# Routing statistics by groups of four tiles in a macaron MoE and attention block

## The chip, the cores and the metric

The kernel runs on one core of one Trainium2 chip. The metric is the device time of one execution in microseconds. PE is TensorE, DVE is VectorE, ACT is ScalarE, POOL is GpSimd, SP is SyncE; SP and ACT also issue DMAs.

## The reference

4096 tokens of width 256 go through a macaron block: x + 0.5 FFN(norm x), then x + attention(norm x), then x + 0.5 FFN(norm x) again with the same weights. The norm has no weights:

```python
m = jnp.mean(x, axis=axis, keepdims=True)
v = jnp.var(x, axis=axis, keepdims=True)
return (x - m) / jnp.sqrt(v + eps)
```

The FFN is a mixture of experts: sigmoid scores over 8 experts from a gate, the top 2 with weights normalised and scaled by 2.5, each expert a gated SiLU network with 176 hidden units, and a shared network of 352 hidden units on every token.

```python
scores = jax.nn.sigmoid(xf @ gate_w.T)
topk_w, topk_idx = jax.lax.top_k(scores, TOP_K)
shared_out = jax.nn.silu(xf @ shared_wg.T) * (xf @ shared_wu.T) @ shared_wd.T
```

## The kernel before

The tokens stand in SBUF as X, 32 tiles of 128 tokens. Each of the two feed-forward parts has three stages with barriers between them: front_stage (routing), expert_stage, combine_stage. The attention lies between the two parts. The change is in front_stage, so it acts twice, from 18.7 us and from 983.9 us of the span.

When front_stage begins, the statistics ST of every tile (bn_stats) are there. The stage turns them into means and variances MV (bn_aggr), adds EPS, takes the square root on ScalarE (L355, in place in RSTD) and the reciprocal on VectorE. Then it works on groups of four tiles, q = 0 to 7:

- normalise(q), VectorE, L476: four tensor_scalar write the normalised tiles into XN. XN has two buffers, so from q = 2 on it waits until TensorE has transposed group q - 2 (xT_done) and until that group's DMA to DRAM has landed (xn_out).
- transpose_x(q, j), TensorE, L650: two tiles each into PSUM. It waits for x_low of the group before (xl_done).
- x_high(q, j), ScalarE, L361, rounds the transposed tiles to fp32r; x_low(q, j), VectorE, L482, takes the remainder.
- keep_xn(q), L366, is a DMA that ScalarE issues behind x_high(q, 1): 512 KB of normalised tiles to DRAM for the expert stage.
- logits(q), turn_logits(q) on TensorE and copy_logits(q) on ScalarE (L373) make the gate's scores, with the gate's weights split by VectorE into GWhl and GWh0 (L457 to L461).
- up(w, m), silu(w, m) (L381), gated_h(w, m) (L490), h_high(w, m) (L393), h_low compute the shared network for the first two groups, one chunk of 128 hidden units in each turn of the loop from q = 2 on (q = 3 on for h_high).
- expert_high(n) (L400, L402) on ScalarE and expert_low(n) (L331) on GpSimd split the experts' weights; L426, L428 and L317, L321 do the same for the shared weights. SP's load of expert n waits until expert_low(n - 2) is done.

Each engine runs its own list in the order in which it is written, and a wait in the list holds all that stands behind it on that engine. ScalarE's list is, for each q: h_high(q - 3), x_high(q, 0), x_high(q, 1), keep_xn(q), copy_logits(q - 1), at q = 1 the shared weights, from q = 2 on expert_high(q - 2) and silu(q - 2). VectorE's list: gate weights, all 32 bn_aggr, add, reciprocal, normalise(0), normalise(1), constants() (L508 to L513, a few casts, OFF, and a memset), and then for each q: x_low(q, 0), x_low(q, 1), normalise(q + 2), at q = 5 h_low_2, from q = 2 on gated_h(q - 2). link(ins) makes VectorE wait until that instruction is done. OFF is read only by the combine stage.

Of the kernel before, what the change touches and what calls it, by code (L numbers as in the profile page):

```python
# [11 lines left out]
ALU = mybir.AluOpType  # L12
ACT = mybir.ActivationFunctionType
AX = mybir.AxisListType
F32 = mybir.dt.float32
# [12 lines left out]
EPS = 1e-5  # L28
# [96 lines left out]
def front_stage(nc, tag, S, X, ST, MV, ident, w_up, w_down, w_shared, gate, xn_dram,  # L125
# [6 lines left out]
    D, NT, NS, FF, E, NJ = S.D, S.NT, S.NS, S.FF, S.E, S.NJ  # L132
    FA, FB = S.FA, S.FB
    NG = NT * TOP_K
    NW = NT // 4
# [10 lines left out]
    with ExitStack() as c1:  # L146
# [12 lines left out]
        GW = sb("GW", [P, 2, E])  # L159
# [191 lines left out]

        @block.scalar
        def _(act):
            act.wait_ge(rstd_in, 1)
            nc.scalar.activation(RSTD[:, :], RSTD[:, :], ACT.Sqrt).then_inc(rstd_out, 1)  # L355

            def x_high(q, j):
                act.wait_ge(xT_done, 2 * q + j + 1)
                if q >= NF + 2:
                    act.wait_ge(lt_done, q - 1)  # L360
                nc.scalar.activation(x_part(0, q)[:, :, j * 2 * P:(j + 1) * 2 * P],  # L361
                                     ps_x[j][:, :].rearrange("p (c n) -> p c n", c=2), ACT.Copy).then_inc(xh_done, 1)

            def keep_xn(q):
                act.wait_ge(xn_ready, 4 * q + 4)
                act.dma_start(xn_dram[q * 4 * P:(q + 1) * 4 * P, :].rearrange("(i p) d -> p i d", p=P),  # L366
                              XN[:, q % 2, :, :]).then_inc(xn_out[q % 2], 16)

            def copy_logits(q):
                act.wait_ge(lt_done, q + 1)  # L370
                if q >= 2:
                    act.wait_ge(gate_done, q - 1)
                nc.scalar.activation(LT[0:2 * E, q % 2, :], ps_lt[q % 2][0:2 * E, :], ACT.Copy).then_inc(lt_copied, 1)  # L373

            def silu(w, m):
                n = HC * w + m
                act.wait_ge(up_done, 2 * n + 1)

                if n >= 2:
                    wait_low(n - 2)  # L380
                nc.scalar.activation(H[0:CHUNKS[m][1], n % 2, :], ps_u[2 * n % RING][0:CHUNKS[m][1], :],  # L381
                                     ACT.Silu).then_inc(silu_done, 1)

            def wait_low(n):
                if n % HC == 2:
                    act.wait_ge(hl_dve, n // HC + 1)
                else:
                    act.wait_ge(hl_pool, 2 * (n // HC) + n % HC + 1)

            def h_high(w, m):  # L390
                n = HC * w + m
                act.wait_ge(h_ready, n + 1)
                nc.scalar.activation(hs[0][0:CHUNKS[m][1], w, m, :], H[0:CHUNKS[m][1], n % 2, :],  # L393
                                     ACT.Copy).then_inc(hh_done, 1)

            def expert_high(n):
                e, b = n, n % 2
                block_free(act, e)
                act.wait_ge(expert_in[b], 16 * 3 * (n // 2 + 1))
                nc.scalar.activation(W[:, e, S.UH:S.UH + 4 * FF], raw[b][:, 0:4 * FF], ACT.Copy).then_inc(expert_hi, 1)  # L400
                for at_h, at, rows_n, to in ((S.AH, RA, FA, 0), (S.BH, RB, FB, 0), (S.BH, RB, FB, FB)):
                    nc.scalar.activation(W[to:to + rows_n, e, at_h:at_h + D], raw[b][0:rows_n, at:at + D],  # L402
                                         ACT.Copy).then_inc(expert_hi, 1)

            def token_ids(n):

                act.wait_ge(onehot, n + 1)
                if n >= 2:
                    act.wait_ge(tok_done, n - 1)
                for g in range(CH):  # L410
                    last = nc.scalar.activation(TSEL[:, n % 2, g, :], EQT[:, n % 2, g, :], ACT.Copy,
                                                scale=id_f[:, n * CH + g:n * CH + g + 1])
                last.then_inc(ids, 1)

            for q in range(NW):
                if q >= 3:
                    h_high(*divmod(q - 3, HC))
                x_high(q, 0)
                x_high(q, 1)
                keep_xn(q)  # L420
                if q >= 1:
                    copy_logits(q - 1)
                if q == 1:
                    act.wait_ge(shared_in, SHARED_IN)
                    for c in range(2):
                        nc.scalar.activation(WU[0][:, c, :, :], raw_up[:, c, :, :], ACT.Copy).then_inc(shared_hi, 1)  # L426
                    for m, (at, n) in enumerate(CHUNKS):
                        nc.scalar.activation(WS[0][0:n, m, :], raw_down[0:n, m, :], ACT.Copy).then_inc(shared_hi, 1)  # L428
                if q >= 2:
                    expert_high(q - 2)  # L430
                    silu(*divmod(q - 2, HC))
            h_high(NF - 1, HC - 1)
            copy_logits(NW - 1)
            act.wait_ge(gate_done, NW)
            act.wait_ge(shared_lo, 2 + HC)
            nc.scalar.activation(SC[:, :, :].rearrange("p t e -> p (t e)"), ps_gate[:, 0:E * NT],
                                 ACT.Sigmoid).then_inc(sig_done, 1)
            for n in range(NW - 2, E):
                expert_high(n)
            act.wait_ge(pre_done, 1)  # L440
            nc.scalar.activation(PRE[:, :], ps_count[:, 0, :], ACT.Copy).then_inc(pre_copied, 1)
            nc.scalar.activation(TOT[:, :], ps_count[:, 1, :], ACT.Copy).then_inc(pre_copied, 1)
            for n in range(8):
                token_ids(n)

        @block.vector
        def _(dve):
            count = [0]

            def link(ins):  # L450

                count[0] += 1
                ins.then_inc(chain, 1)
                dve.wait_ge(chain, count[0])

            dve.wait_ge(gate_in, 16)
            nc.vector.memset(GWh0[:, :, E:2 * E].bitcast(F32), 0.0)  # L457
            nc.vector.tensor_copy(GWh0[:, :, 0:E], GW[:, :, :])
            nc.vector.tensor_tensor(ADD[:, :], ident[0:2 * E, 0:E], ident[0:2 * E, E:2 * E], ALU.add)
            link(nc.vector.tensor_copy(GWhl[:, :, 0:E], GW[:, :, :]))  # L460
            nc.vector.tensor_tensor(GWhl[:, :, E:2 * E], GW[:, :, :], GWhl[:, :, 0:E].bitcast(F32),  # L461
                                    ALU.subtract).then_inc(gate_w, 1)
            for t in range(NT):
                last = nc.vector.bn_aggr(MV[:, t, :], ST[:, t, :])
            link(last)
            nc.vector.tensor_scalar(RSTD[:, :], MV[:, :, 1], EPS, None, ALU.add).then_inc(rstd_in, 1)
            dve.wait_ge(rstd_out, 1)
            link(nc.vector.reciprocal(RSTD[:, :], RSTD[:, :]))

            def normalise(q):  # L470
                if q >= 2:
# [34 lines left out]
            def constants():  # L506
                dve.wait_ge(consts, 6)
                link(nc.vector.tensor_copy(prio[:, :], prio_i[:, :]))  # L508
                link(nc.vector.tensor_copy(row_f[:, :], row_i[:, :]))
                link(nc.vector.tensor_copy(row_h[:, :], row_i[:, :]))  # L510
                link(nc.vector.tensor_copy(id_f[:, :], id_i[:, :, :].rearrange("p k t -> p (k t)")))
                nc.vector.scalar_tensor_tensor(OFF[:, :], MV[:, :, 0], -1.0, RSTD[:, :], ALU.mult, ALU.mult)
                nc.vector.memset(W[FB:2 * FB, :, S.BL:S.BL + D].bitcast(F32), 0.0).then_inc(cleared, 1)  # L513
                dve.wait_ge(cleared, 1)

# [76 lines left out]
            def one_hot(n):  # L592
                if n >= 2:
# [6 lines left out]
                                        RF[:, part].unsqueeze(2).to_broadcast([P, CH, P]),  # L600
                                        ALU.is_equal).then_inc(rows, 1)

            normalise(0)
            normalise(1)
            constants()
            for q in range(NW):
                x_low(q, 0)
                x_low(q, 1)
                if q + 2 < NW:
                    normalise(q + 2)  # L610
                if q == 5:
                    h_low_2(0)
                if q >= 2:
                    gated_h(*divmod(q - 2, HC))
# [28 lines left out]
        def _(pe):  # L643
# [72 lines left out]
                                            start=n == 0 and g == 0, stop=n == 7 and g == CH - 1)  # L716
                last.then_inc(tok_done, 1)

            pe.wait_ge(gate_w, 1)
            for q in range(NW):  # L720
                transpose_x(q, 0)
                transpose_x(q, 1)
                if q >= 1:
                    logits(q - 1)
                if q >= 2:
                    turn_logits(q - 2)
                if q == 2:
                    pe.wait_ge(shared_lo, 2)
                if q >= 2:
                    up(*divmod(q - 2, HC))  # L730
# [1392 lines left out]
```

## Time and profile before

| | us |
|---|---|
| median of three runs | 1339.91 |
| lowest, highest | 1338.66, 1339.95 |
| the profiled execution | 1341.68 |
| its span, first to last instruction | 1339.6 |
| TensorE, VectorE, ScalarE, GpSimd busy | 1163.8, 982.0, 793.1, 535.3 |

Times in rows are microseconds from the start of the span. Busy shares are means over stages with different limits; what matters for one stage is the order of its instructions in time and which wait ends last.

### The profile page before, as it was taken

Reading aid. Unit: us, or ns where it says so; the run is one execution under the profiler, and the core shown is the slowest. Engines: PE = TensorE matmul, PEld = TensorE weight load, DVE = VectorE, ACT = ScalarE, POOL = GpSimd, SP = SyncE. Lnnn points to the kernel's source line nnn. Section 1 sums busy time; section 2 is a strip of 40 time slices with the busy share of each in tenths; the row PEclk is TensorE's granted clock in tenths of the full one; section 3 lists DMA queues with packets and bytes.
Section 4 is the critical chain, followed back from the end, with each engine's and each line's share of the span. In section 5 each row is a group of like instructions: output and inputs, shape, how many; then the busy total and the mean of one; then the engine's idle time right before and its main releaser. Section 6 shows DMA issues by size and latency. Waiting matters only on the chain. (4 is left out here: it accounts for less than half of the span.)

```text
span 1339.6 us, 38859 instructions
## 1 busy us (share of the span) xinstructions
PE 1163.8 (87%) x13796; PEld 866.7 (65%) x13796; DVE 982.0 (73%) x2151; ACT 793.1 (59%) x1944; POOL 535.3 (40%) x738
## 2 busy tenths in 40 slices
PE   1873999989859969999998999999858659999897
PEld 1653999968748825555554555553746559999686
DVE  6666666648869879998887888893586766666586
ACT  1645666663226606877776777788636466666631
POOL 0642444337715512322332322333516334442576
PEclk9975999989969969999998999999979769999899
DMA  6320444423355651222221222210234114443354
GB/s 206 127 80 28 128 132 134 125 74 95 96 190 196 220 92 47 67 59 62 60 63 52 62 59 60 63 39 3 95 113 128 49 56 131 131 134 111 99 150 137
DMA packets 96384, 132.43 MB, mean 99 GB/s; under 512 B 15644, under 2 KB 81116, under 8 KB 96220
## 3 DMA queue, kind: packets, MB, share of 16 engines
q1 hardware_dynamic: 74716, 86.07, 21.4%
q0 software_dynamic: 13056, 35.67, 9.7%
q10 hardware_dynamic: 8448, 8.39, 1.8%
q8 instruction: 117, 1.92, 0.6%
q14 instruction: 47, 0.39, 0.1%
HBM read 81.35 MB, written 48.23 MB: 97 GB/s over the span
## 5 line engine op out<-in xcount | busy, mean ns | idle before, releaser
L1740 ACT ACTIVATE s_PR<-s_ps_b 128x512 f32<-128x512 f32 (+3 forms) x768 | 331.1, 496 | 123.2 <-PE s_ps_b L1851 118.1
L1760 DVE TENSOR_REDUCE s_MX<-s_ps_a 128x1 f32<-128x512 f32 (+3 forms) x608 | 357.9, 653 | 50.4 <-PE s_ps_a L1829 47.3
L1851 PE MATMUL s_ps_b<-QO,KO 99*32 99x512 bf16 (+3 forms) x3072 | 217.2, 329 | 8.1 <-issue 3.6
L1711 POOL TENSOR_SCALAR_AFFINE_SELECT s_PR<-s_PR 128x256 f32<-128x256 f32 x256 | 103.2, 406 | 301.7 <-ACT s_PR L1740 296.1
L792 POOL DMA_INDIRECT f_XG<-xn_scratch,f_tok_u x144 | 136.1, 945 | 206.2 <-PE f_ps_x L888 137.7
L1829 PE MATMUL s_ps_a<-KO,QO 96*32 96x512 bf16 (+3 forms) x3072 | 212.2, 338 | 1.4 <-DVE s_MX L1760 1.2
L1003 POOL DMA_INDIRECT f_YG<-y_scratch,f_slots_u x128 | 128.3, 1003 | 87.4 <-issue 33.8
L1868 PE MATMUL s_ps_o<-s_PR,s_VG 128*17 128x512 f32 (+3 forms) x1536 | 158.8, 488 | 1.0 <-POOL s_PR L1711 0.6
L898 PE MATMUL f_ps_u<-f_W,f_xh 128*128 x576 | 152.8, 348 | 0.0
L1851 PEld LDWEIGHTS s_ps_b<-QO,KO 99*32 99x32 bf16 x3072 | 81.3, 96 | 90.7 <-ACT s_PR L1740 44.4
L1829 PEld LDWEIGHTS s_ps_a<-KO,QO 96*32 96x32 bf16 x3072 | 81.2, 99 | 69.3 <-DVE s_MX L1760 24.6
L920 PE MATMUL f_ps_y<-f_W,f_hh 112*128 (+1 forms) x576 | 121.1, 303 | 0.6 <-DVE f_hh L852 0.4
L1824 PE MATMUL s_ps_a<-s_neg,s_identb 128*32 128x128 bf16 (+2 forms) x1408 | 92.5, 251 | 9.7 <-POOL s_identb L1676 9.4
L845 DVE TENSOR_TENSOR f_xl<-f_ps_x,f_xh 128x256 fp32r<-128x256 f32 x144 | 61.1, 424 | 51.9 <-ACT f_xh L817 51.9
L898 PEld LDWEIGHTS f_ps_u<-f_W,f_xh 128*128 128x128 f32 x576 | 95.4, 193 | 0.4 <-issue 0.4
L898 PE MATMUL f_ps_u<-f_W,f_xl 128*128 x288 | 94.3, 327 | 0.0
L864 DVE TENSOR_TENSOR f_H<-f_SG,f_ps_u 128x176 f32<-128x176 f32 x144 | 48.6, 338 | 58.0 <-ACT f_SG L832 58.0
L920 PEld LDWEIGHTS f_ps_y<-f_W,f_hh 112*128 112x128 f32 (+1 forms) x576 | 88.0, 190 | 1.6 <-issue 1.6
L832 ACT ACTIVATE f_SG<-f_ps_u 128x176 f32<-128x176 f32 x144 | 45.8, 318 | 67.8 <-PE f_ps_u L898 67.8
L811 ACT ACTIVATE f_YS<-f_ps_y 128x256 f32<-128x256 f32 x144 | 55.5, 386 | 37.2 <-PE f_ps_y L920 37.2
L888 PE MATMUL f_ps_x<-ident,f_XG 128*128 128x128 f32 x288 | 56.6, 279 | 11.8 <-DMA f_XG<-xn_scratch,f_tok_u 11.8
L650 PE MATMUL f_ps_x<-ident,f_XN 128*128 128x128 f32 x128 | 21.7, 317 | 50.3 <-DVE f_XN L476 33.9
(227 smaller groups left out, 2637.8 us busy)
## 6 DMA issues: line engine op xcount, KB each, us to landing
y_scratch<-f_YS SPq DMA_DIRECT2D x144, 128.0 KB, 1.7
qk_scratch<-p_QK SPq DMA_DIRECT2D x32, 384.0 KB, 3.1
QO<-qk_scratch SPq DMA_DIRECT2D x96, 128.0 KB, 2.8
KO<-qk_scratch SPq DMA_DIRECT2D x96, 128.0 KB, 2.8
xn_scratch<-f_XN ACTq DMA_DIRECT2D x16, 512.0 KB, 4.0
f_RAW<-in_w_up SPq DMA_DIRECT2D x16, 352.0 KB, 3.2
X<-in_x SPq DMA_DIRECT2D x4, 1024.0 KB, 9.4
x_scratch<-X SPq DMA_DIRECT2D x1, 4096.0 KB, 16.4
```

The source lines that it names most:

```text
L792: nc.gpsimd.indirect_dma_start(out=XG[:, j % 4, :], out_offset=None, in_=xn_dram[:, :], in_offset=bass.IndirectOffsetOnAxis(ap=tok_u[:, j: ...
L845: nc.vector.tensor_tensor(xs[1][:, k % 2, :], ps_x[k % 2][:, 0:D], xs[0][:, k % 2, :].bitcast(F32), ALU.subtract).then_inc(xl_done, 1)
L898: last = nc.tensor.matmul(ps_u[k % 2][:, 0:2 * FF], xs[a][:, k % 2, c * P:(c + 1) * P], W_at[:, ds(offset + ((S.UL if b else S.UH) + c * 2 ...
L920: last = nc.tensor.matmul(ps_y[b][:, 0:D], h, W_at[0:h.shape[0], ds(offset + at, D)], start=i == 0, stop=i == len(plan) - 1)
L1003: nc.gpsimd.indirect_dma_start(out=YG[:, t % RING, c, :], out_offset=None, in_=y_dram[:, :], in_offset=bass.IndirectOffsetOnAxis(ap=slots_ ...
L1711: nc.gpsimd.affine_select(out=tile, in_=tile, compare_op=ALU.is_ge, fill=0.0, base=0, pattern=[[0, 2], [1, P]], channel_multiplier=-1)\
L1740: nc.scalar.activation(PR[:, u // 2 % SLOTS, u % 2, 0:W - lo], ps_b[u % RING][:, lo:W], ACT.Exp, scale=SCALE).then_inc(exp_done, 1)
L1760: nc.vector.tensor_reduce(MX[:, h:h + heads, i, s], ps_a[slot][:, 0:heads * keys].rearrange("p (h n) -> p h n", h=heads), AX.X, ALU.max).t ...
L1824: nc.tensor.matmul(scores[strip, :, keys - P:keys], identb[:, strip], neg[:, 0:heads, :], start=True, stop=False, skip_group_check=True)
L1829: last = nc.tensor.matmul(ps_a[slot][strip, at:at + keys], QO[k][0:R, h, i * P + strip.start:i * P + strip.stop], KO[k][0:R, h, s * W:s * ...
L1851: last = nc.tensor.matmul(ps_b[u % RING][strip, lo:W], KO[k][0:RM, h, i * P + strip.start:i * P + strip.stop], QO[k][0:RM, h, hf * W + lo: ...
L1868: last = nc.tensor.matmul(ps_o[32 * h:32 * h + V1, lo:W], VG[k][:, i, h * V1:(h + 1) * V1], PR[:, (2 * n + h // 2) % SLOTS, h % 2, 0:W - l ...
```

## The change

The aggregations, the added EPS, the square root and the reciprocal are done for four tiles at a time: measure(q) on VectorE, deviation(q) on ScalarE, invert(q) on VectorE. Groups 0 and 1 are measured before the first normalisation. The gate's weights are prepared behind normalise(0) and group 2 is measured behind them; groups 3 to 7 are measured inside the loop, behind x_low(q, 1): group 3 at q = 0, groups 4 and 5 at q = 1, groups 6 and 7 at q = 2. ScalarE takes deviations 0 and 1 ahead of its loop, deviation 2 at q = 0, 3 and 4 at q = 1, 5, 6 and 7 at q = 2, each time behind x_high(q, 1) and ahead of keep_xn(q). TensorE waits for the gate's weights behind the transposes of q = 1 and no longer at its start. OFF is computed at q = 6 and no longer in constants().

```diff
 @block.scalar
+            def deviation(q):
+                act.wait_ge(rstd_in, q + 1)
+                cols = RSTD[:, 4 * q:4 * q + 4]
+                nc.scalar.activation(cols, cols, ACT.Sqrt).then_inc(rstd_out, 1)
-            act.wait_ge(rstd_in, 1)
-            nc.scalar.activation(RSTD[:, :], RSTD[:, :], ACT.Sqrt).then_inc(rstd_out, 1)
...
+            deviation(0)
+            deviation(1)
             for q in range(NW):
...
                 x_high(q, 0)
                 x_high(q, 1)
+                for n in ((2,), (3, 4), (5, 6, 7))[q] if q < 3 else ():
+                    deviation(n)
                 keep_xn(q)
 @block.vector
+            def measure(q):
+                tiles = range(4 * q, 4 * q + 4)
+                for t in tiles:
+                    last = nc.vector.bn_aggr(MV[:, t, :], ST[:, t, :])
+                link(last)
+                nc.vector.tensor_scalar(RSTD[:, 4 * q:4 * q + 4], MV[:, 4 * q:4 * q + 4, 1], EPS, None,
+                                        ALU.add).then_inc(rstd_in, 1)
+            def invert(q):
+                dve.wait_ge(rstd_out, q + 1)
+                cols = RSTD[:, 4 * q:4 * q + 4]
+                link(nc.vector.reciprocal(cols, cols))
...
-                nc.vector.scalar_tensor_tensor(OFF[:, :], MV[:, :, 0], -1.0, RSTD[:, :], ALU.mult, ALU.mult)
...
+            measure(0)
+            measure(1)
+            invert(0)
             normalise(0)
+            gate_weights()
+            measure(2)
+            invert(1)
             normalise(1)
             constants()
             for q in range(NW):
                 x_low(q, 0)
                 x_low(q, 1)
+                for n in ((3,), (4, 5), (6, 7))[q] if q < 3 else ():
+                    measure(n)
                 if q + 2 < NW:
+                    invert(q + 2)
                     normalise(q + 2)
+                if q == NW - 2:
+                    nc.vector.scalar_tensor_tensor(OFF[:, :], MV[:, :, 0], -1.0, RSTD[:, :], ALU.mult, ALU.mult)
 @block.tensor
-            pe.wait_ge(gate_w, 1)
             for q in range(NW):
                 transpose_x(q, 0)
                 transpose_x(q, 1)
+                if q == 1:
+                    pe.wait_ge(gate_w, 1)
```

gate_weights() holds the five instructions of L457 to L461 with their wait for the gate's DMA.

## Rows read from the trace of the kernel before

**Rows 1.** Timeline, VectorE, first routing stage: start us, us, instruction, idle before and its releaser.

```profile
20.57 0.15 DVE L458 CAST f_GWh<-f_GW 128x16 fp32r<-128x16 f32 x1 [2.37 <-issue]
...
20.99 2.21 DVE L464 BATCH_NORM_AGGREGATE MV<-ST 128x2 f32<-128x6 f32 x32
...
23.71 0.35 DVE L468 RECIPROCAL f_RSTD<-f_RSTD 128x32 f32<-128x32 f32 x1 [0.29 <-ACT f_RSTD L355]
24.10 2.67 DVE L476 TENSOR_SCALAR f_XN<-X,MV,f_RSTD 128x256 f32<-128x256 f32 x8
...
27.63 0.19 DVE L512 SCALAR_TENSOR_TENSOR f_OFF<-MV,f_RSTD 128x32 f32<-128x32 f32 x1
28.29 1.76 DVE L513 MEMSET f_W<- 64x2048 f32 x1 [0.47 <-issue]
30.09 1.29 DVE L482 TENSOR_TENSOR f_W<-f_ps_x,f_W 128x512 fp32r<-128x512 f32 x2
31.66 1.38 DVE L476 TENSOR_SCALAR f_XN<-X,MV,f_RSTD 128x256 f32<-128x256 f32 x4 [0.29 <-DMA xn_scratch<-f_XN]
```

**Rows 2.** Timeline, ScalarE and its DMA queue (ACTq), same stage.

```profile
18.68 1.28 ACT L355 ACT_TABLE_LOAD   x1 [18.68 <-PEq L2059]
...
26.10 0.60 ACT L361 ACTIVATE f_W<-f_ps_x 128x512 fp32r<-128x512 f32 x1 [2.43 <-PE f_ps_x L650]
...
26.96 0.40 ACTq L366 DMA_DIRECT2D xn_scratch<-f_XN  x1
...
32.91 0.37 ACTq L366 DMA_DIRECT2D xn_scratch<-f_XN  x1
34.47 0.59 ACT L373 ACTIVATE f_LT<-f_ps_y 16x512 f32<-16x512 f32 x1 [0.97 <-PE f_ps_y L661]
...
35.35 0.37 ACTq L366 DMA_DIRECT2D xn_scratch<-f_XN  x1
```

**Rows 3.** DMA issues at 18.68, 26.96 and 32.91: count, KB, us to landing.

```profile
f_GW<-in_gate SPq DMA_DIRECT2D x1, 8.0 KB, 1.8
...
xn_scratch<-f_XN ACTq DMA_DIRECT2D x1, 512.0 KB, 4.6
...
xn_scratch<-f_XN ACTq DMA_DIRECT2D x1, 512.0 KB, 2.9
```

**Rows 4.** Timeline, GpSimd and VectorE, 35.9 to 45.8 us.

```profile
35.89 3.38 POOL L317 TENSOR_TENSOR f_WUl<-f_RAWS,f_WUh 128x704 fp32r<-128x704 f32 x2 [15.88 <-ACT f_WUh L426]
...
35.94 4.99 DVE L476 TENSOR_SCALAR f_XN<-X,MV,f_RSTD 128x256 f32<-128x256 f32 x4 [1.70 <-DMA xn_scratch<-f_XN]
...
37.65 1.77 DVE L476 TENSOR_SCALAR f_XN<-X,MV,f_RSTD 128x256 f32<-128x256 f32 x1
...
39.23 2.30 POOL L321 TENSOR_TENSOR f_WSl<-f_RAWS,f_WSh 128x256 fp32r<-128x256 f32 x3
40.85 1.27 DVE L482 TENSOR_TENSOR f_XT<-f_ps_x,f_XT 128x512 fp32r<-128x512 f32 x2
41.49 3.21 POOL L331 TENSOR_TENSOR f_W<-f_RAW,f_W 128x704 fp32r<-128x704 f32 x3
42.05 3.13 DVE L476 TENSOR_SCALAR f_XN<-X,MV,f_RSTD 128x256 f32<-128x256 f32 x4
45.10 0.67 DVE L490 TENSOR_TENSOR f_H<-f_H,f_ps_u 128x512 f32<-128x512 f32 x1
```

**Rows 5.** Timeline, ScalarE and its DMA queue, 38.6 to 46 us.

```profile
38.68 0.77 ACT L400 ACTIVATE f_W<-f_RAW 128x704 fp32r<-128x704 f32 x1
...
40.52 1.28 ACT L381 ACT_TABLE_LOAD   x1
...
45.82 0.41 ACTq L366 DMA_DIRECT2D xn_scratch<-f_XN  x1
```

**Rows 6.** Timeline, VectorE, second routing stage.

```profile
989.14 2.67 DVE L476 TENSOR_SCALAR f_XN<-X,MV,f_RSTD 128x256 f32<-128x256 f32 x8
...
1010.29 0.67 DVE L490 TENSOR_TENSOR f_H<-f_H,f_ps_u 128x512 f32<-128x512 f32 x1
```

More of the change, by code:

```diff
@@ L454, in link, with gate_weights @@
                 dve.wait_ge(chain, count[0])
[L456 to L468, printed above, removed]
+            def gate_weights():
+                dve.wait_ge(gate_in, 16)
+                nc.vector.memset(GWh0[:, :, E:2 * E].bitcast(F32), 0.0)
+                nc.vector.tensor_copy(GWh0[:, :, 0:E], GW[:, :, :])
+                nc.vector.tensor_tensor(ADD[:, :], ident[0:2 * E, 0:E], ident[0:2 * E, E:2 * E], ALU.add)
+                link(nc.vector.tensor_copy(GWhl[:, :, 0:E], GW[:, :, :]))
+                nc.vector.tensor_tensor(GWhl[:, :, E:2 * E], GW[:, :, :], GWhl[:, :, 0:E].bitcast(F32),
+                                        ALU.subtract).then_inc(gate_w, 1)
+            def measure(q):
[9 more added lines that the diff above has]
+                link(nc.vector.reciprocal(cols, cols))
             def normalise(q):
```

## The prediction

> **What bounds the kernel now.** I read the page first: TensorE is busy 87% of the span, but the kernel is a series of stages with barriers between them, and the change touches only the first part of the routing stage, which runs twice (from 18.7 us and from 983.9 us). What a saving is worth has to be read there. I therefore took the timeline of VectorE in that stage [rows 1], then ScalarE's with its DMA queue [rows 2], the landing times of its DMAs [rows 3], and VectorE beside GpSimd where both are busy [rows 4].
>
> The reader should see three things. First, the opening is one serial chain: gate weights, 32 aggregations, add, square root, reciprocal, and only at 24.10 the first normalised tile [rows 1]. Second, from the second group on, VectorE waits for a write of xn to DRAM, because XN has two buffers: normalise(3) starts at 35.94 after 1.70 us of idle, released by the DMA that keep_xn(1) issued at 32.91 [rows 2, 4]. Third, normalise(3) and normalise(4) run beside GpSimd's subtractions and are slow: 4.99 us and 3.13 us for four tiles [rows 4], where eight tiles took 2.67 us at the start [rows 1]. The four single tiles keep step with GpSimd's operations (one of them takes 1.77 us, 37.65 to 39.42, beside an L317 operation of about 1.7 us) [rows 4]. From gated_h(0,0) at 45.10 on the stage is a loop: h_high and keep_xn(3) leave at 45.82, the write lands, VectorE normalises, multiplies, ScalarE rounds, and the next write leaves [rows 4, 5]. So what the change does to the start of gated_h(0,0) is what it does to the stage; nothing behind that point gets shorter.
>
> **The start of the stage.** The opening no longer needs all 32 tiles. An aggregation costs 2.21/32 = 0.07 us each in a row [rows 1], so four are 0.2 us plus some 0.15 us of drain; with the add (OFF's 32 columns take 0.19 us [rows 1], four about 0.16) a measure(q) is about 0.5 us, from 0.35 if the drain is covered to 0.7. VectorE can have measure(0) done at about 19.35, but ScalarE's table load runs from 18.68 to 19.96 [rows 2], so the square root, for which VectorE waited 0.29 us before [rows 1], is through at about 20.2 and, with a reciprocal of 0.15 to 0.35 us [rows 1], normalise(0) starts at about 20.4 instead of 24.10: 3.7 us earlier. Four things now stand between it and x_low(0): the gate weights (20.57 to 20.99, 0.42 us [rows 1]), measure(2) 0.5 us, invert(1) 0.2 us; OFF (0.19 us [rows 1]) leaves. x_low(0,0) moves from 30.09 to about 27.4, 2.7 us earlier. The gate weights themselves need their DMA, landed 1.8 us after its issue at 18.7 [rows 3], long before 21.7, and the matmuls that read them come only behind the second transposes, so their move costs just its 0.42 us. OFF at q = 6 falls into idle time of VectorE and costs nothing; were that cover gone it would cost its 0.19 us.
>
> Then q = 0: two x_low (1.2 us), measure(3) 0.5, invert(2) 0.2, and normalise(2) at 29.4. It needs the write of keep_xn(0). That issue moves from 26.96 to about 23.3 (x_high(0,0) was 2.0 us after the first normalised tile, and still is [rows 1, 2]), in the thick of the weight loads. It took 4.6 us before [rows 3], which gives 27.9; sharing the engines with more of the weights I allow 28 to 31.5, the last being the time at which the same write landed before. I take about 28.7: hidden. normalise(2) takes 1.3 us, x_low(1) 1.2 us, and VectorE is at 31.9.
>
> **Where the gain goes.** At q = 1 ScalarE's program has deviation(4) ahead of keep_xn(1), and deviation(4) waits for measure(4), which VectorE reaches only after x_low(1,1). ScalarE's queue is in order, so keep_xn(1), copy_logits(0) and the rounding of the shared weights stand behind it. measure(4) is done at 32.4, keep_xn(1) leaves at about 32.5 against 32.91. At 2.9 us to landing [rows 3] and a hop, normalise(3) starts at 35.5 instead of 35.94. The 2.7 us have become 0.4. The other branch keeps more: copy_logits(0) at 32.6 instead of 34.47 [rows 2], so GpSimd's L317 starts at 34.05 instead of 35.89 [rows 4], 1.85 us earlier, and up(0,0) with it. Because GpSimd is ahead, normalise(3) meets only the tail of the first L317 operation, the second (1.7 us) and two of L321 (0.77 each): 0.4 + 1.7 + 0.8 + 0.8 = 3.6 us instead of 4.9, and x_low(2,0) begins at 39.1 instead of 40.85.
>
> At q = 2 the same thing comes in a heavier form. Before, keep_xn(2) left at 35.35, because ScalarE's sequencer ran ahead of its engine [rows 2], and its landing was never waited for: normalise(4) followed x_low(2) at 42.05 without idle [rows 4]. Now deviation(6) and deviation(7) stand in front of it and wait for measure(6) and measure(7), which stand behind normalise(3) and x_low(2,1). x_low(2) 39.1 to 40.3, two measures 1.1 us, so deviation(7) and keep_xn(2) go at about 41.4: 6 us later than before. Landing 2.9 us and a hop: normalise(4) at 44.4 instead of 42.05. Behind the same two deviations stand copy_logits(1), expert_high(0) (38.68 to 40.5, 1.85 us), the table load for Silu (1.28 us) and silu(0,0), which followed its table load at 41.8 [rows 5] and now starts at about 45.2. expert_high(0) feeds GpSimd's expert_low(0), so that moves from 41.49 [rows 4] to about 42.95 and runs to 46.15. normalise(4) is therefore still beside it: last tile at 46.6. gated_h(0,0) starts at 46.55 against 45.10 (the silu, ending 45.8, is just ahead). **Sum: +1.45 us in the first stage.** As one sum from normalise(4)'s start: +2.35 us for the write, and -0.9 us because it meets less of GpSimd's work.
>
> The second stage has the same rows at another offset: first tile at 989.14, gated_h(0,0) 21.15 us behind it at 1010.29 [rows 6], where the first stage has 21.00 [rows 1, 4]. The same steps give normalise(0) at 985.6, keep_xn(1) at 997.65, keep_xn(2) at 1006.5, gated_h at about 1011.7: +1.4 us. Behind that point, invert(q) for q = 5 to 7 falls in VectorE's wait for the write and is free. Together +2.9 us.
>
> A rule weighed: the Trainium skill, page "SBUF — State Buffer", section "Who interferes with whom", says that a VectorE instruction in a 2-port mode and a GpSimd instruction exclude each other, and the one that issues first holds the ports to its end. The trace agrees on the exclusion (1.77 us for a tile beside a 1.7 us subtraction [rows 4]). By the rule's second half a normalise that comes in between two GpSimd operations would be held for a whole one, as in the next paragraph's late case; if instead every normalise got in first it would lose nothing, and gated_h would wait for the silu alone, 0.8 us a stage instead of 1.45, which is the wash below.
>
> **Bounds of the size.** Per stage: if normalise(4) is not held by GpSimd, gated_h follows the silu at 45.9 and the loss is 0.8 us. If keep_xn(1) lands 0.3 us later, normalise(3) meets one more long subtraction: +0.7, so 2.1. If keep_xn(0) lands only at 31.5, the opening's gain is gone before q = 1, normalise(3) ends at 40.9 as before, keep_xn(2) leaves at 43.2 and gated_h is at 48.4: +3.3. Twice these: +1.6 to +6.6 us.
>
> **Rivals.** *The head start survives* (faster). ScalarE's deviations 4, 6 and 7 would have to find their numbers ready. Then x_low(0)'s 2.7 us go through to normalise(3) and gated_h(0,0), less 0.2 us for each measure on VectorE in q = 1 and 2: about -2 us a stage, -4 in all, 1336. For it: the opening is truly serial, and DVE is idle 1.70 us before normalise(3) [rows 4]. Against it: the wait is on work that by VectorE's order comes after x_low. It decides if deviation(7) is through before about 38, 3 us ahead of my reckoning. *A wash*: the two sides cancel within the bound, that is a loss of under 1.3 us per stage; the 0.8 us case and smaller measures lead here, about 1341. *The late write*: keep_xn(0) loses to the weight loads, +3.3 us per stage, about 1346.5. *The change does nothing*: the opening is not on the path. Against it stands a chain without a gap down to the first x_high, which waited for the transposes [rows 1, 2]; I give it no share of its own.
>
> **How the numbers follow.** The sum is against the profiled execution, 1341.68 us (span 1339.6 and 2.1 us around it): 1344.6. The profiled run is 1.8 us above the median 1339.91 of three runs; the same +2.9 us on the median gives 1342.8. A measurement of this kernel can tell about 0.2%, 2.7 us, so my value lies only just beyond. Chances: the stalled queue at its reckoned size or above 0.42 (0.37 of it over the bound, 0.05 just under), the late write 0.13, a wash 0.31, the head start surviving 0.14. Slower by over 0.2%: 0.37 + 0.13 = 0.50; within: 0.31 + 0.05 = 0.36; faster: 0.14. Range 1337.5 to 1346.5: the upper end takes in the late write, the lower end cuts the full gain of the head start and keeps a part of it.
>
> **What would show it.** Right: normalise(0) near 20.4; keep_xn(1) issued about 0.4 us earlier than before, not 2.7; keep_xn(2) issued at 41 or later instead of 35.35; ScalarE idle 3 to 5 us ahead of a square root, released by VectorE's add; normalise(4) released by the DMA; gated_h(0,0) 1 to 2 us later than 45.10 and 1010.29, with the loops behind unchanged. Wrong: if deviation(6) and (7) follow their x_high at once, or if normalise(4) starts before 42. The weak steps are the landing of keep_xn(0), the phase of normalise(3) against GpSimd, and the length of a measure.

## The result, and the profile after

| | before | after |
|---|---|---|
| median of 5 runs, us | 1339.95 | 1348.10 |
| lowest, highest | 1338.66, 1341.60 | 1344.86, 1349.01 |
| the profiled execution (span) | 1341.68 (1339.6) | 1348.10 (1346.4) |
| ratio after / before, 95% interval | | 1.0052 (1.0035 to 1.0068) |

The change makes the kernel slower, by 7.0 us (4.7 to 9.1) by the ratio; the two medians differ by 8.15 us. The forecast had the direction, and not the size: 1342.8, with a range that ended at 1346.5.

VectorE, first stage, timeline of the changed kernel; these lines answer to [rows 1, 4]:

```profile
20.50 1.39 DVE L491 TENSOR_SCALAR f_XN<-X,MV,f_RSTD 128x256 f32<-128x256 f32 x4
...
27.44 1.29 DVE L497 TENSOR_TENSOR f_W<-f_ps_x,f_W 128x512 fp32r<-128x512 f32 x2
...
29.98 1.38 DVE L491 TENSOR_SCALAR f_XN<-X,MV,f_RSTD 128x256 f32<-128x256 f32 x4 [0.68 <-DMA xn_scratch<-f_XN]
...
36.16 3.82 DVE L491 TENSOR_SCALAR f_XN<-X,MV,f_RSTD 128x256 f32<-128x256 f32 x4 [2.55 <-DMA xn_scratch<-f_XN]
39.90 1.28 DVE L497 TENSOR_TENSOR f_XT<-f_ps_x,f_XT 128x512 fp32r<-128x512 f32 x2
...
45.24 2.38 DVE L491 TENSOR_SCALAR f_XN<-X,MV,f_RSTD 128x256 f32<-128x256 f32 x4 [3.01 <-DMA xn_scratch<-f_XN]
47.54 0.67 DVE L505 TENSOR_TENSOR f_H<-f_H,f_ps_u 128x512 f32<-128x512 f32 x1
```

ScalarE and its DMA queue, same stretch; they answer to [rows 2, 5]:

```profile
33.08 0.20 ACT L357 ACTIVATE f_RSTD<-f_RSTD 128x4 f32<-128x4 f32 x1 [2.13 <-DVE f_RSTD L477]
33.09 0.37 ACTq L368 DMA_DIRECT2D xn_scratch<-f_XN  x1
...
41.70 0.20 ACT L357 ACTIVATE f_RSTD<-f_RSTD 128x4 f32<-128x4 f32 x1 [4.29 <-DVE f_RSTD L477]
42.19 0.20 ACT L357 ACTIVATE f_RSTD<-f_RSTD 128x4 f32<-128x4 f32 x1 [0.28 <-DVE f_RSTD L477]
42.19 0.37 ACTq L368 DMA_DIRECT2D xn_scratch<-f_XN  x1
```

The first tile comes 3.6 us earlier, x_low(0,0) 2.65 us earlier. Then ScalarE stands 2.13 us before deviation(4) and 4.29 us before deviation(6), each time released by VectorE's add, and the write behind it leaves at once when it is through: the third one at 42.19 instead of 35.35. gated_h(0,0), which the forecast took as the mark of the stage, starts at 47.54 instead of 45.10.

Below, that mark is counted from the stage's first GpSimd instruction, so that executions can be compared: its start (L490 before, L505 after) less the start of the first IOTA. It is +26.31 and +26.39 us in the two stages before, +28.68 and +29.62 after: 2.37 and 3.23 us later.

### The profile page after: what moved, and what is told of

The parts are those of the page before. It is cut to its first block and busy times, and to the rows that moved or that the text cites. A ratio compares the mean times of both kernels' runs of the same rounds, so it can differ in the third digit from the quotient of the medians.

```text
span 1346.4 us, 38901 instructions
## 1 busy us (share of the span) xinstructions
PE 1168.2 (87%) x13796; PEld 867.7 (64%) x13796; DVE 982.8 (73%) x2179; ACT 795.3 (59%) x1958; POOL 534.3 (40%) x738
## 3 DMA queue, kind: packets, MB, share of 16 engines
q8 instruction: 117, 1.92, 0.6%
## 5 line engine op out<-in xcount | busy, mean ns | idle before, releaser
L858 ACT ACTIVATE f_SG<-f_ps_u 128x176 f32<-128x176 f32 x144 | 45.8, 318 | 69.1 <-PE f_ps_u L924 68.9
```

## The experiments

In one table first. Ratios are to runs of the kernel before in the same set. There are four sets, A to D, on different chips or at different times, in which the kernel before took 1339.95, 1339.71, 1369.71 and 1339.11 us (medians), so times are compared inside a set only. The marks are from one profile each.

| kernel | set | ratio (95%) | mark, stage 1 | mark, stage 2 |
|---|---|---|---|---|
| before | A | 1 | 26.31 | 26.39 |
| after | A | 1.0052 (1.0035 to 1.0068) | 28.68 | 29.62 |
| write_first | B | 0.9988 (0.9978 to 0.9997) | 24.69 | 24.67 |
| measure_early | B | 1.0001 (0.9990 to 1.0012) | 25.62 | 25.78 |
| both | B | 0.9982 (0.9973 to 0.9991) | 25.04 | 24.59 |
| gate_only | B | 0.9979 (0.9968 to 0.9991) | 24.66 | 24.80 |
| after_again | C | 1.0070 (1.0041 to 1.0100) | 28.75 | 30.15 |
| after_held | C | 1.0057 (1.0032 to 1.0082) | 27.95 | 28.74 |
| gate_held | C | 1.0000 (0.9977 to 1.0023) | 24.54 | 24.72 |
| both_bias | C | 0.9977 (0.9955 to 1.0000) | 23.61 | 23.60 |
| first_stall_gone | D | 1.0027 (1.0014 to 1.0041) | 27.47 | 27.24 |
| both_bias_held | D | 0.9961 (0.9947 to 0.9975) | 23.30 | 23.68 |

**write_first: the writes ahead of the square roots.**

```diff
-                for n in ((2,), (3, 4), (5, 6, 7))[q] if q < 3 else ():
-                    deviation(n)
                 keep_xn(q)
+                for n in ((2,), (3, 4), (5, 6, 7))[q] if q < 3 else ():
+                    deviation(n)
```

> The changed kernel, with keep_xn(q) put ahead of the deviations in ScalarE's list. Theory (writes queued behind the square roots): keep_xn(1) leaves near 30.3 instead of 33.09 and keep_xn(2) near 36 instead of 42.19; normalise(3) starts near 33.6 and is done before GpSimd starts, normalise(4) no longer waits for a write; silu(0,0) is still late (about 43), so gated_h(0,0) near 43.6 instead of 47.54. Time about 3 us below the kernel before, 1336 to 1338. Rival (ScalarE's own idle time ahead of the square roots is what costs, through expert_high and silu): gated_h(0,0) stays above 46 and the time near 1346.

keep_xn(1) left at 30.17, keep_xn(2) at 33.45, and gated_h(0,0) started at 43.46, behind a silu that was still late (VectorE waited 2.60 us for it). The loss turns into a gain with one line moved: the time is 1.6 us under the kernel before, where about 3 were expected. ScalarE still stands still before deviations 4, 6 and 7, for 1.92, 1.64 and 0.48 us. So most of the loss came with the writes queued behind the square roots; the late silu is what the idle time still costs.

**measure_early and first_stall_gone: one stall at a time.** The first measures groups 6 and 7 at q = 1, so that the stall at q = 2 goes; the second takes deviation(4) at q = 2, so that the one at q = 1 goes.

```diff
-                for n in ((3,), (4, 5), (6, 7))[q] if q < 3 else ():
+                for n in ((3,), (4, 5, 6, 7))[q] if q < 2 else ():
                     measure(n)
```

> The changed kernel, with groups 6 and 7 measured at q = 1, where VectorE waits for a write, instead of q = 2; ScalarE's list is unchanged. The stall at q = 1 stays, that at q = 2 goes. Theory: keep_xn(1) still near 33.1, keep_xn(2) leaves near 35, normalise(4) follows x_low(2) at about 41.2, silu(0,0) near 41.5, gated_h(0,0) near 44.1. Time 1337 to 1341, so the stall at q = 2 alone accounts for 3 us a stage or more. Rival (the opening's rearrangement and the shorter instructions cost by themselves): the time stays above 1344.

```diff
-                for n in ((2,), (3, 4), (5, 6, 7))[q] if q < 3 else ():
+                for n in ((2,), (3,), (4, 5, 6, 7))[q] if q < 3 else ():
                     deviation(n)
```

> The changed kernel, with deviation(4) taken at q = 2 instead of q = 1, so that only the stall at q = 1 goes and the one at q = 2 stays. If the two stalls add up, each taking its own part, about 1 to 1.5 us a stage come back and gated_h(0,0) lies near 27.3 behind the start, time 2 to 3 us under the changed kernel. If they form one chain in which GpSimd's subtractions decide (normalise(3) is done ahead of them once keep_xn(1) leaves at 30.3), keep_xn(2) leaves near 39.3, normalise(4) starts near 42.3, gated_h(0,0) comes near 25.4, that is 3 us a stage, as much as removing the stall at q = 2 gave.

By the marks, the stall at q = 2 is worth 3.06 and 3.84 us in the two stages, the one at q = 1 1.21 and 2.38. In the second stage both figures take in a write of the changed kernel that landed late (4.5 us, see below). In the first the two add up to 4.27 us, and write_first, without blocked writes, is 3.99 us earlier. So they add up roughly, as the first reading had it, and the picture of one chain that either would break is wrong. That picture failed on normalise(3), which did not start at 33.6 ahead of GpSimd but at 34.81, held behind an add, and ran 3.87 us beside the subtractions.

**both: no write behind a wait.** keep_xn(q) ahead of the deviations, deviations 4 to 7 at q = 2, groups 4 to 7 measured at q = 1.

> The changed kernel, with keep_xn(q) ahead of the deviations, groups 4 to 7 measured at q = 1 and deviations 4 to 7 taken at q = 2, so that no square root waits. Theory: the head start of about 2.7 us reaches gated_h(0,0), near 42.4 against 45.10 before; 2 to 2.7 us a stage, time about 1335 (1334 to 1337). Rival (the head start is lost to the landing of keep_xn(0), which has to share with the weight loads, and to GpSimd's share of VectorE's ports): gated_h(0,0) at 44 to 45 and the time within 2 us of 1340.

The ratio, 0.9982, is 2.4 us under the kernel before, where about 5 were expected, and the square roots of groups 6 and 7 still waited, for 0.80 and 0.49 us. VectorE beside GpSimd in its first stage:

```profile
33.31 1.50 DVE L477 TENSOR_SCALAR f_RSTD<-MV 128x4 f32<-128x4 f32 x1
34.72 0.36 DVE L475 BATCH_NORM_AGGREGATE MV<-ST 128x2 f32<-128x6 f32 x4
35.12 1.31 DVE L477 TENSOR_SCALAR f_RSTD<-MV 128x4 f32<-128x4 f32 x1
...
37.24 3.96 DVE L491 TENSOR_SCALAR f_XN<-X,MV,f_RSTD 128x256 f32<-128x256 f32 x4
```

```profile
33.07 3.33 POOL L317 TENSOR_TENSOR f_WUl<-f_RAWS,f_WUh 128x704 fp32r<-128x704 f32 x2 [13.07 <-ACT f_WUh L432]
```

An add of four numbers per partition takes 0.17 us alone and 1.50 and 1.31 us here: like a tile of normalise, it lasts until GpSimd's operation beside it ends (the two of L317 take 3.33 us from 33.07 on). The aggregations in between keep their 0.36 us. The Trainium skill, page "SBUF — State Buffer", section "Who interferes with whom", says that tensor_scalar can enter a mode that takes the ports shared with GpSimd, and that an instruction with one input outside those modes does not contend. The trace agrees on the add, at 1.50 us; the 0.36 us of the aggregation, which has one input, fit the second half.

**both_bias: without those adds.** EPS becomes the bias of ScalarE's square root, which reads MV.

```diff
-                link(last)
-                nc.vector.tensor_scalar(RSTD[:, 4 * q:4 * q + 4], MV[:, 4 * q:4 * q + 4, 1], EPS, None,
-                                        ALU.add).then_inc(rstd_in, 1)
+                last.then_inc(rstd_in, 1)
...
-                nc.scalar.activation(cols, cols, ACT.Sqrt).then_inc(rstd_out, 1)
+                nc.scalar.activation(cols, MV[:, 4 * q:4 * q + 4, 1], ACT.Sqrt, bias=EPSB[:, 0:1]).then_inc(rstd_out, 1)
```

> The kernel of the run called both, with EPS added by ScalarE as the bias of the square root, so that measure(q) is four aggregations and no tensor_scalar. Theory: in that run the adds of groups 5 to 7 stood 1.5, 1.3 and 0.4 us beside GpSimd's subtractions, so VectorE reached normalise(3) at 37.2; without them at 34 to 34.5, and gated_h(0,0) 1.5 to 2 us earlier than 25.0 behind the start, near 23.2; time about 1334. Rival (GpSimd holds normalise(3) anyway, whenever it starts): gated_h(0,0) within 0.7 us of that run's, time near 1337.

normalise(3) at 33.68 instead of 37.24, the mark at 23.61 instead of 25.04. Most of the 3.6 us is given back to GpSimd (normalise(3) took 4.54 us instead of 3.96, normalise(4) 2.92 instead of 1.38), and 1.4 and 1.0 us a stage stay. The time is 0.9977 of before; against the kernel both the runs can't tell it apart.

**gate_only: the other part of the change alone.** The kernel before, with the five instructions for the gate's weights behind normalise(0) and TensorE's wait for them at q = 1.

> The kernel before, with one part of the change alone: the gate's weights are prepared behind normalise(0), and TensorE waits for them at q = 1. Theory: the opening waited for the gate's DMA, so the aggregations start at 18.8 instead of 20.99, normalise(0) near 21.95 instead of 24.10 and x_low(0,0) near 28.4 instead of 30.09; 1 to 1.7 us a stage, time 1336.5 to 1338. Rival (a late write of keep_xn(0) takes it back, landing at 31 or later): under 1 us in all.

normalise(0) at 21.87, x_low(0,0) at 28.31, the mark 1.65 and 1.59 us earlier, and 2.8 us in all. So moving the gate's weights alone gives as much as the runs write_first or both, which have the groups of four as well: marks of 24.66 and 24.80 beside 24.69 and 24.67, 25.04 and 24.59. VectorE's lines show where this head start was held up (normalise(2) waits until 31.78, 31.66 before) and that normalise(3) starts at 34.28 instead of 35.94 all the same:

```profile
31.78 1.38 DVE L469 TENSOR_SCALAR f_XN<-X,MV,f_RSTD 128x256 f32<-128x256 f32 x4 [2.18 <-DMA xn_scratch<-f_XN]
33.08 1.28 DVE L475 TENSOR_TENSOR f_W<-f_ps_x,f_W 128x512 fp32r<-128x512 f32 x2
34.28 5.03 DVE L469 TENSOR_SCALAR f_XN<-X,MV,f_RSTD 128x256 f32<-128x256 f32 x4
```

**after_again, after_held, gate_held, both_bias_held: the landing of the early write.** after_again is the changed kernel unaltered; its loss came again (1.0070), with marks of 28.75 and 30.15. The other three hold SP's loads of experts 0 and 1 until keep_xn(0) and keep_xn(1) have landed:

```diff
             for n in range(E):
+                if n < 2:
+                    sp.wait_ge(xn_out[n], 16)
                 load_expert(n)
```

> The changed kernel once more, for a second profile. If the 4.5 us that keep_xn(1) took to land in the second stage belongs to the kernel (its place among the other DMAs), it comes again; if it is a chance event, keep_xn(1) lands in 2.9 us there too and gated_h(0,0) comes near 28.7 us behind that stage's start instead of 29.6. Time 1346 to 1348 either way.

> The changed kernel, with SP's loads of experts 0 and 1 held until keep_xn(0) and keep_xn(1) have landed. Theory: keep_xn(0) took 6.5 us because it shares the DMA engines with those loads; now it lands in 3 to 4.5 us, normalise(2) follows invert(2) near 29.4 without idle, and keep_xn(1), behind deviation(4), leaves near 32.5. gated_h(0,0) 0.5 to 1.3 us a stage earlier than in the changed kernel, time about 1346. Rival (the early write costs nothing further down): gated_h(0,0) stays at 28.7 behind the start.

> The kernel with the gate's weights moved alone, and the same hold on SP's expert loads. normalise(2) should come near 29.6 instead of 31.78. But keep_xn(1) leaves with x_high(1,1) at 31.1 in any case and lands 2.9 us later, so normalise(3) stays near 34.2 and gated_h(0,0) near 24.7 behind the start: no gain, time within 1.5 us of the kernel with the gate's weights moved. If the late landing of keep_xn(0) is what limits that kernel, it gains 1 to 2 us a stage instead.

> The run both_bias with SP's expert loads held until keep_xn(0) and keep_xn(1) have landed: the version that all findings point to. normalise(2) near 28.9 instead of 29.94, normalise(3) near 33.1 (behind the landing of keep_xn(1), issued near 30) instead of 33.68, gated_h(0,0) 23.0 to 23.6 behind the start against 23.6: 0 to 0.6 us a stage, time 0.2 to 0.4% under the kernel before. If GpSimd's subtractions alone set normalise(3)'s end, nothing is gained over both_bias.

keep_xn(0) of the first stage, in the changed kernel and in after_held:

```profile
xn_scratch<-f_XN ACTq DMA_DIRECT2D x1, 512.0 KB, 6.5
```

```profile
xn_scratch<-f_XN ACTq DMA_DIRECT2D x1, 512.0 KB, 3.6
```

With the experts' loads out of its way (those of the shared weights still run beside it) it lands in 3.6 us, normalise(2) starts at 29.19 without idle, keep_xn(1) at 32.30 and the mark is at 27.95 instead of 28.7: 0.8 us of the loss in the first stage is this. In time the 0.8 us can't be seen (1.0057 beside 1.0070, intervals wide on that chip). In gate_held the idle time before normalise(2) is gone too (29.58) and the mark does not move (24.54 beside 24.66), since keep_xn(1) leaves behind x_high(1,1) in any case. Its marks are 1.77 and 1.67 us before those of the kernel before, yet the time is level, 1.0000 (0.9977 to 1.0023); with an interval of 3 us to either side this neither shows a gain nor rules out gate_only's. both_bias_held gained 0.3 us in the first stage (23.30 beside 23.61) and nothing in the second (23.68 beside 23.60), but it is the fastest measured, 0.9961, 5.2 us (3.4 to 7.1) under the kernel before. It was timed on another chip than both_bias, and the intervals overlap, so that the hold itself gains anything is not shown.

## Why the prediction was off

**The mechanism** of the loss was right, and three steps of the working were off. ScalarE's queue stood before deviations 4 and 6, the write keep_xn(2) went out at 42.19 (forecast 41.4, at 35.35 before), normalise(4) became bound by the DMA. write_first removes the blocked writes and the loss with them; after_held leaves both stalls in and stays slow.

**The start** was right to 0.1 us: normalise(0) 20.50 (20.4), x_low(0,0) 27.44 (27.4). gate_only shows that 2.2 of the 3.6 us belong to the gate's weights (normalise(0) at 21.87 instead of 24.10): before, VectorE waited 2.37 us for their DMA with all else behind it.

**First failed step: "I take about 28.7: hidden"** for the landing of keep_xn(0). It took 6.5 us instead of the 5.4 that this means, and 6.7 us in the second stage. normalise(2) started at 29.98, not 29.4, and everything behind it was later than forecast, by 0.6 to 1.0 us: keep_xn(1) 33.09 (32.5), GpSimd's L317 34.92 (34.05), x_low(2) 39.90 (39.1), gated_h 47.54 (46.55). after_held gives this term back: its mark is 1.64 us behind before's, against the forecast of 1.45. My own bound (28 to 31.5) held the landing, at about 29.8, but between the two ends I stood too near the good one, though the row was a write that had shared with fewer loads.

**Second failed step: "the same steps give" for the second stage.** keep_xn(1) landed there in 4.5 us, not 2.9, so that normalise(3) started 19.15 us behind the stage's start instead of 17.3; normalise(3), at 2.89 us, got 0.9 of it back. The view of DMAs over 1001.6 to 1006.4 shows, in 40 slices, what the bytes did:

```profile
DMA  0000008079999999999961000000000000000000
GB/s 0 0 0 0 0 0 137 17 247 341 324 350 324 324 341 316 341 333 316 324 197 26 9 9 9 17 26 26 26 26 17 26 26 26 9 0 0 0 0 0
...
q8 instruction: 1, 0.02, 2.2%
```

One packet of the instruction queue goes just ahead of the write; nearly all of the write is done in 13 slices, and a tail at 9 to 26 GB/s, on average about one sixteenth of the 324 to 350 GB/s before it, holds the semaphore back for another 1.7 us. The same packet and tail are in the second stage of after_again (3.7 us) and after_held (4.4), and on keep_xn(2) in the runs write_first (3.9) and both (3.8). In measure_early (3.8) the packet is there too, and the next write hides a tail. In gate_only the packet goes about 1.2 us ahead, and keep_xn(2) lands in 3.2. In the kernel before it comes only at the end of keep_xn(1), which lands in 2.9. That the packet is the cause fits every one of these, but was not tried by an experiment.

**Third failed step: "what the change does to the start of gated_h(0,0) is what it does to the stage".** The marks are 5.6 us later in sum, the time 7.0 (4.7 to 9.1). In the profiles the expert stage begins, counted from its front stage's start, 2.41 and 4.81 us later than before. So the first stage keeps its mark's 2.37, and the second loses another 1.6 us behind its mark of 3.23. There it is TensorE's clock. The last matmuls of up() in the second stage, kernel after, by windows (PEclk is the granted clock):

```profile
core 0: us, PE busy (x) PEld busy (x) DVE busy (x) ACT busy (x) POOL busy (x), PEclk, DMA share, GB/s
1037.00:1043.00 6.00, 4.14 (x22) 3.08 (x21) 4.31 (x9) 3.04 (x7) 2.43 (x4) 1.00 0.58 178
1043.00:1048.00 5.00, 5.00 (x18) 3.34 (x16) 1.97 (x3) 4.20 (x10) 4.17 (x5) 0.54 0.37 107
```

and the same piece of work in the kernel before:

```profile
1037.00:1042.00 5.00, 5.00 (x26) 3.30 (x25) 1.98 (x3) 4.22 (x9) 4.19 (x5) 1.00 0.43 120
```

At the upper level (2.4 GHz) a matmul of this line takes 0.39 us, at the lower (1.2 GHz) 0.63, and VectorE's last gated_h waits for the chunk. Kernel before, then after:

```profile
1038.87 0.39 PE L684 MATMUL f_ps_u<-f_W,f_WUl 128*96 128x512 f32 x1
1043.14 0.68 DVE L490 TENSOR_TENSOR f_H<-f_H,f_ps_u 96x512 f32<-96x512 f32 x1 [2.01 <-ACT f_H L381]
```

```profile
1046.82 0.63 PE L709 MATMUL f_ps_u<-f_W,f_WUl 128*96 128x512 f32 x1
1051.21 0.68 DVE L505 TENSOR_TENSOR f_H<-f_H,f_ps_u 96x512 f32<-96x512 f32 x1 [3.66 <-PE f_ps_u L709]
```

In the first stage both kernels have a granted clock of 0.67 there. Whether the change causes the other is open: this wait of the second stage is 3.66 and 3.64 us in the runs both and both_bias, which have no blocked write, and 2.0 us in write_first, measure_early, first_stall_gone and gate_only, one profile each.

**Added up**, on the profiles: 2.85 us were forecast for the two stages. The landings of keep_xn(0) add 1.6 (the marks of the changed kernel less those of after_held: 0.73 and 0.88), the rest of the marks 1.1, nearly all of it in the second stage, where keep_xn(1) landed late, and what lies behind the mark there 1.6. That is 7.2 us, beside the 7.0 of the ratio.

**The rivals.** *The head start survives* took place wherever the stalls were removed, at 1.3 to 3.0 us a stage. *A wash* did not take place in the changed kernel; it did in measure_early, with the stall at q = 1 alone left (1.0001). *The late write* was real in part: its price, by after_held, is 0.7 and 0.9 us in the two stages here, not 3.3.

## What to carry to other kernels

The head start here came for the larger part from moving a wait for a DMA out of the opening (gate_only), and not from cutting the batch: try the small move by itself first. When a batch is cut into pieces and spread over a pipelined loop, each new handshake is a wait in the middle of another engine's list. Look at what stands behind it there, above all at DMA issues: before, the engine's sequencer ran ahead and sent them early, and that goes with the first wait. Put issues ahead of such waits, and do the small pieces a turn before they are wanted, but not with instructions that share ports with a busy GpSimd. And take the duration of a transfer from a row with the same neighbours, not from the same transfer at another time.

## What the runs showed of the hardware

- A VectorE tensor_scalar on 128x4 numbers took 0.17 us alone, and 1.50 us beside a GpSimd subtraction of 128x704; four bn_aggr took 0.36 us beside it and 0.37 alone.
- In one row it did not help VectorE to be first. Kernel before, second stage, the timeline of VectorE and of GpSimd:

```profile
1001.00 1.92 DVE L476 TENSOR_SCALAR f_XN<-X,MV,f_RSTD 128x256 f32<-128x256 f32 x1 [1.73 <-DMA xn_scratch<-f_XN]
```

```profile
1001.08 1.69 POOL L317 TENSOR_TENSOR f_WUl<-f_RAWS,f_WUh 128x704 fp32r<-128x704 f32 x1 [15.95 <-ACT f_WUh L426]
```

VectorE started 0.08 us ahead and yet lasted to 1002.92, past GpSimd's end at 1002.77. The Trainium skill, page "SBUF — State Buffer", section "Who interferes with whom", says that whichever issues first holds the ports to its end. By that rule the tile would have taken the 0.41 us of a tile alone. GpSimd's spans in a profile are rough, so this is a doubt and no disproof.
- A 512 KB write to DRAM from ScalarE's queue landed in 2.9 us alone, in 4.6 us issued at 26.96 behind most of the weight loads, and in 6.3 to 7.0 us issued at 23.2 to 24.7 among them (first stages).
